# Two of five graph passes: VectorE's part written out, one comparison for four one-hots, waits by fours, eight PSUM banks

## What is computed

```python
# layer 0 (the reference multiplies by the matrix first; the kernel sums first and multiplies then)
support = x @ hamilton
msgs = edge_weight[:, None] * support[edge_src]
out = jax.ops.segment_sum(msgs, edge_dst, num_segments=N)
# layer 4
msg = xw[src] * norm[:, None]
out = jax.ops.segment_sum(msg, dst, num_segments=N) + b
```

## Time and profile before

| | us |
|---|---|
| median of 3 timed executions | 6917.32 (6915.71 to 6927.64) |
| the profiled execution, from first to last instruction | 8185.9 |
| busy in it: PE / PEld | 4889.8 / 3073.8 |
| busy in it: DVE / ACT / POOL | 4369.9 / 2515.7 / 4642.4 |

### The profile page before, as it was taken

The page is one execution under the profiler, slowest core; times in us unless marked ns, Lnnn a source line. Parts: engine busy times, 40 slices in busy tenths (PEclk is TensorE's granted clock), DMA queues, the critical chain, the costliest instruction groups (busy, mean ns, idle before and its releaser), DMA issues. The chain is left out here.

```text
span 8185.9 us, 104343 instructions
## 1 busy us (share of the span) xinstructions
PE 4889.8 (60%) x17264; PEld 3073.8 (38%) x17265; DVE 4369.9 (53%) x11401; ACT 2515.7 (31%) x7600; POOL 4642.4 (57%) x5272
## 2 busy tenths in 40 slices
PE   3555555967777777836565556455555563554555
PEld 1322333534444444624343334233333342332333
DVE  4444444657777777735555556344444452443446
ACT  0000000347777777634444446111111130000003
POOL 5666666445555555556666664555555536666661
PEclk6666666967667777867676678566666676666666
DMA  2323234366666666543333343333333343332234
GB/s 78 89 86 87 86 89 83 125 193 201 194 200 202 196 199 201 138 125 108 106 109 105 103 108 81 95 101 98 100 94 97 95 118 89 88 89 85 86 88 88
DMA packets 499271, 962.78 MB, mean 118 GB/s; under 512 B 105402, under 2 KB 296605, under 8 KB 491711
## 3 DMA queue, kind: packets, MB, share of 16 engines
q0 software_dynamic: 240064, 696.46, 31.0%
q1 hardware_dynamic: 258845, 263.03, 10.4%
HBM read 895.84 MB, written 64.63 MB: 117 GB/s over the span
## 5 line engine op out<-in xcount | busy, mean ns | idle before, releaser
L1026 PE MATMUL bank<-ring,ohc 128*128 128x256 f32 (+3 forms) x8800 | 3440.9, 538 | 2067.8 <-issue 668.3
L1026 PEld LDWEIGHTS bank<-ring,ohc 128*128 128x128 f32 x8800 | 2047.9, 258 | 3233.8 <-issue 1852.1
L1509 DVE TENSOR_TENSOR acc<-acc,bank 128x256 f32 (+2 forms) x3520 | 1483.0, 421 | 1992.4 <-issue 910.1
L711 POOL DMA_INDIRECT ring<-g_t,stage x1760 | 1738.9, 988 | 1149.1 <-PE bank L1026 600.0
L711 POOL DMA_INDIRECT ring<-kv_t,stage x880 | 850.4, 966 | 798.9 <-PE bank L1026 478.2
L711 POOL DMA_INDIRECT ring<-in_x,stage x880 | 835.0, 949 | 483.5 <-issue 229.9
L711 POOL DMA_INDIRECT ring<-xs_t,stage x880 | 834.1, 948 | 473.2 <-issue 227.9
L826 ACT ACTIVATE ring<-ring 128x32 f32<-128x32 f32 x3520 | 754.4, 306 | 15.0 <-issue 14.9
L795 ACT ACTIVATE ohc<-iota,rel_c 128x128 f32<-128x128 f32 x1760 | 564.2, 388 | 183.4 <-PE bank L1026 130.9
L849 ACT ACTIVATE cl<-cl 128x1 f32<-128x1 f32 (+3 forms) x111 | 22.5, 203 | 1863.3 <-issue 883.7
L1506 DVE SCALAR_TENSOR_TENSOR acc<-acc,aux,bank 128x264 f32 x880 | 419.8, 477 | 83.8 <-PE bank L1026 42.7
(11 more groups left out here) (309 smaller groups left out, 5433.5 us busy)
## 6 DMA issues: line engine op xcount, KB each, us to landing
aux<-relb_t SPq DMA_DIRECT2D x56, 1024.0 KB
aux<-q_t SPq DMA_DIRECT2D x880, 64.0 KB
relx<-relb_t SPq DMA_DIRECT2D x55, 512.0 KB
ring<-g_t,stage POOLq DMA_INDIRECT x1760
x<-ring SPq DMA_DIRECT2D x21, 896.0 KB, 4.2
ring<-x SPq DMA_DIRECT2D x21, 896.0 KB, 9.4
mk<-mk SPq DMA_DIRECT2D x445, 32.1 KB
ring<-in_x,stage POOLq DMA_INDIRECT x880
```

The lines of the kernel that those rows point to most:

```text
L711: g_.indirect_dma_start(out=rings[L][:, slot, 0:W], out_offset=None, in_=table[L][:, :], in_offset=bass.IndirectOffsetOnAxis(ap=stage[:, s ...
L1026: return mm(agp[k % AB][:, 0:width], ohc[:, hot, :], rg[:, slot, vo:vo + width], start=True, stop=True)
L1509: tt(win, win, agp[k % AGP[L]][:, 0:width], ALU.add).then_inc(p["added"], 1)
```

## The change

It touches the passes of layers 0 and 4 on DVE and PE. DVE's part is no longer a loop: 220 groups of four tiles are written out, with constant addresses and wait values (only the window's offset still comes from a register). One TENSOR_TENSOR compares `iota` with four columns of `rel_c` and makes four one-hots (128x512). In layer 0 a second one multiplies them by four columns of `ew_c`, after a wait on a new semaphore, `compared`. DVE waits for the matmuls of a group at once, makes the comparison of the group two ahead, adds the four windows and then, in layer 0, multiplies. `LEAD` is now 2 groups instead of 3 tiles, and all 16 buffers of `ohc` are in use. PE keeps its loop and waits by groups for one-hots and banks; it uses eight banks instead of four. In the other layers only the counts of `added` are shifted by four.

```diff
-LEAD = 3
+LEAD = 2
...
-    return sum(TS[m] + LEAD for m in range(L) if HEADS[m] == 0)
+    return sum(TS[m] // 4 for m in range(L) if HEADS[m] == 0)
...
-        AGP = [4, 3, 4, 4, 4]
+        AGP = [8, 3, 4, 4, 8]
...
                         for k in range(G):
-                            pe.wait_ge(p["wready"], b * G + (k + 1 + made_before(L)))
                             slot = rset * G + k
                             if k % 4 == 0:
+                                pe.wait_ge(p["wready"], b * (G // 4) + (k // 4 + 1 + made_before(L)))
                                 pe.wait_ge(s_ring[slot // 4], i * 64 + (64 + ring_base(L, slot // 4)))
-                            pe.wait_ge(p["added"], b * G + (k + 1 + summed(L)))
-                            window_sum(slot, k % 8, k).then_inc(p["agg"], 1)
+                                pe.wait_ge(p["added"], b * G + (k + 4 + summed(L)))
+                            window_sum(slot, k % OHS, k).then_inc(p["agg"], 1)
...
-                    dve.sem_inc(p["added"], 4)
+                    dve.sem_inc(p["added"], 8)
...
                 if not H:
-                    def hot(b, k):
-                        rel = rel_c[:, ds(b * G + k, 1)]
-                        if L == 0:
-                            ins = v.tensor_scalar(ohc[:, k % 8, :], iota[:, :], rel, ew_c[:, ds(b * G + k, 1)],
-                                                  ALU.is_equal, ALU.mult)
-                        else:
-                            ins = v.tensor_scalar(ohc[:, k % 8, :], iota[:, :], rel, None, ALU.is_equal)
-                        ins.then_inc(p["wready"], 1)
...
+                    four = lambda col: col.unsqueeze(2).to_broadcast([128, 4, 128])
+
+                    def hot_four(g):
+
+                        hots = ohc[:, 4 * g % OHS:4 * g % OHS + 4, :]
+                        ins = tt(hots, iota[:, :].unsqueeze(1).to_broadcast([128, 4, 128]),
+                                 four(rel_c[:, 4 * g:4 * g + 4]), ALU.is_equal)
+                        ins.then_inc(s_cmp if L == 0 else p["wready"], 1)
+
+                    def weigh_four(g):
+
+                        hots = ohc[:, 4 * g % OHS:4 * g % OHS + 4, :]
+                        dve.wait_ge(s_cmp, g + 1)
+                        tt(hots, hots, four(ew_c[:, 4 * g:4 * g + 4]), ALU.mult).then_inc(p["wready"], 1)
+
+                    def add_four(g):
+
+                        for k in range(4 * g, 4 * g + 4):
+                            dve.wait_ge(p["added"], k + 8 + summed(L))
+                            win = acc[:, ds(window_at(k // G % 2, k % G), width)]
+                            tt(win, win, banks[k % 8][:, 0:width], ALU.add).then_inc(p["added"], 1)
+                    quads = TS[L] // 4
+                    load_offsets(0, 0, 0)
+                    for g in range(LEAD):
+                        hot_four(g)
+                        if L == 0:
+                            weigh_four(g)
+                    for g in range(quads):
+                        if g % (G // 4) == 1 and (g // (G // 4) + 1) * G < TS[L]:
+                            load_offsets(g // (G // 4) + 1, (g // (G // 4) + 1) % 2, 0)
+                        dve.wait_ge(p["agg"], 4 * g + 4 + 16 * AHEAD[L])
+                        if g + LEAD < quads:
+                            hot_four(g + LEAD)
+                        add_four(g)
+                        if L == 0 and g + LEAD < quads:
+                            weigh_four(g + LEAD)
```

More of the change, by code:

```diff
@@ L350, in gnn_kernel @@
         s_mkst = sem("masks_stored")
+        s_cmp = sem("compared")
         s_same = sem("same_loaded")
@@ L1024, in window_sum @@
                 def window_sum(slot, hot, k):
-                    return mm(agp[k % AB][:, 0:width], ohc[:, hot, :], rg[:, slot, vo:vo + width], start=True, stop=True)
+                    return mm(banks[k % AB][:, 0:width], ohc[:, hot, :], rg[:, slot, vo:vo + width], start=True, stop=True)
                 if not H:
@@ L1058, in add_tiles @@
                                     pe.wait_ge(p["wv"], b * (G // 4) + (weighed(L) + k // 4 + 1))
-                            free = 4 if L == 1 and k == 0 else 5 - AB
+                            free = 8 if L == 1 and k == 0 else 9 - AB
                             pe.wait_ge(p["added"], b * G + (k + free + summed(L)))
@@ L1503, in add_window @@
                     dve.wait_ge(p["agg"], b * G + (k + 1 + 16 * AHEAD[L]))
-                    dve.wait_ge(p["added"], b * G + (k + 4 + summed(L)))
+                    dve.wait_ge(p["added"], b * G + (k + 8 + summed(L)))
                     if L == 1:
@@ L1730, in begin_sums @@
                     def begin_sums(c, off, cp):
-                        dve.wait_ge(p["added"], c * G + (4 + summed(L)))
+                        dve.wait_ge(p["added"], c * G + (8 + summed(L)))
                         dve.wait_ge(p["w"], c + (past(L) + 3))
```

## The result

The changed kernel takes 6962.95 us (6953.71 to 6969.3, four executions) against 6922.05 us for the kernel before beside it: a ratio of 1.0059, interval 1.0047 to 1.0071. It is 0.6% slower, on the side that was forecast and inside the range, but by 41 us where 81 were foretold. A repeat later gave 6962.07 against 6914.35 us, 1.0073 [1.0059, 1.0086].

What follows compares the result with a forecast made beforehand. POOL's gathers were taken to bound both linear passes once DVE doesn't crawl. 6917 us less 30 for the crawl plus 111 for collisions gave 6998 us, 1.2% slower; range 6870 to 7150, the forecast's own 6935 to 7110.

Steps and rivals of the forecast that it cites:

- POOL as the bound: Layers 0 and 4: only POOL's gathers bound the passes if DVE doesn't crawl; DVE and PE work stays hidden, 0 mid-pass.
- The floors: Pass lengths without DVE's crawl, from 880 gathers (1100 us) plus start and end: 1124 us layer 0, 1108 us layer 4.
- The crawl belongs to the profiling: DVE's slow register steps in layers 0 and 4, 479 us when profiled, come from recording; timed kernel keeps 0 to 59.
- The term of -30 us: Layers 0 and 4: the part of DVE's crawl assumed in timed executions, which the change would remove: 30 us.
- the crawl is real: Rival, chance 0.16: DVE crawls in layers 0 and 4 unprofiled too; timed kernel loses 479, pays 111: 6549 us.
- The collision: Layers 0 and 4: wide DVE instructions with two SBUF operands hold POOL's gathers that start inside them: 74 + 37 = 111 us.
- the factor of 0.24 us per us: Gather time lost per us of wide DVE instruction, from layer 2: 69 us on 285 us of L1721.
- Locked in phase: Rival, chance 0.06: every new wide DVE instruction could meet a gather's start, costing 370 us: 7257 us.
- No collision: Rival, chance 0.10: new DVE instructions fall between gather starts or don't hold them: 6887 us, 6858 to 6917.
- the cover is elsewhere: Rival, chance 0.06: POOL's unprofiled pitch is below 1.22 us, PE bounds the pass, collisions cost nothing: 6917 us.

Runs made afterwards that it cites:

- single one-hots: Changed kernel with comparison and multiplication replaced by the old one-hots, one tile each; eight banks, waits by fours and written-out program stay: 6927.83 us, 1.0011 to before.
- the two relatives: Changed kernel with the comparison behind the four adds (0.9897, 0.9872 to before), or split into two of two tiles (0.9899, 0.9904), on chips with the crawl.
- operands in PSUM: Changed kernel with iota and edge weights copied into PSUM banks, so each wide instruction has one SBUF operand; sums share four banks: 6913.38 us, 0.9991 to before.
- the doubled comparison: Changed kernel with each comparison made twice, the second into a buffer that nobody reads: 7030.94 us, 1.0161 to before.
- layer 2's edit: Kernel before with layer 2's L1721 reading weights from their PSUM bank, two preparation steps made ahead of the next scores: 8544.01 us, 1.0152 to before.

## Why the prediction was right, and where not

**POOL as the bound: right.** In the changed kernel POOL waits 7.7 and 0.7 us for PE. Groups of four, late adds and eight banks were to cost nothing in the middle of a pass and up to 3 us at its end. The single one-hots show 4.7 and 2.4 us in all, 2.1 and 1.4 of it at the ends.

**The floors: short by 4 and 18 us.** 1124 and 1108 were forecast, 1128 and 1126 measured. The 55 copies of indices on POOL (11.6 and 11.9 us, `stage` L701) were forgotten, and an end takes 17 us in the kernel before (18 and 20 in the changed one), not 8; in layer 0 the wait of 16.4 us for PE at the start, taken over from the crawling profile, was 5.3.

**"The crawl belongs to the profiling": wrong.** This was the choice on which everything hung. The argument from the two lengths, that an execution 18% longer than the timed ones carries something which these don't, was sound; that this something is the recording was not. The likeliest reading now is that the profile came from a chip with the crawl and the times from one without. Executions without it, profile and all, were seen on two chips, and executions with it on two others. The term of -30 us, what the timed kernel would keep of the crawl, was 0: on the chips of the result there was none to take away. The forecast that the profile would shrink to 7818 us while the time grows was right only in its signs: it shrank to 6958, and the other stages with it.

**The rival "the crawl is real"** (0.16, 6549 us) was nearer the truth than the number of the result says. It holds on two of the four chips; even there the two relatives that were run recover about 1%, not the 5% that it was given; the changed kernel itself wasn't run on such a chip.

**The collision: mechanism right, size 2.2 times too large.** 111 us were forecast, 74 + 37 (worked out exactly, 0.241 us per us gives 73 + 36); the gathers' means say 26 + 21 = 47 against the kernel before, 55 against the same program with operands in PSUM, the excess of the gathers that start inside a wide instruction adds up to 50, and the time says 41 to 50. That the total came as near as 81 against 41 us is partly luck: the 30 us for a crawl that wasn't there took off half of what the collision had too much. The term that failed is the factor of 0.24 us per us, taken over from layer 2 as a whole. Two things are wrong with it.

The smaller one is the form. In layer 2, in the profile from which the forecast was made, gathers that start inside L1721 lose 0.134 us per instruction of the 512 form but 0.346 us per one of the 1024 form, which is 1.8 times as long and makes up almost half of its busy time. By the 512 form alone, the sum would have been 660 x 0.134 = 88 us.

The larger one, the other 38 us or so, is the phase. Each comparison lost 0.09 us in layer 0 and 0.10 in layer 4, each multiplication 0.04, though all have the 512 form's length. In layer 2 POOL and DVE fall into step: held gathers and the instructions of L1721 follow at the same pitch of 1.5 us, and so one gather after another starts at the same place behind an L1721. The rows that follow show it, with 0.29 and 0.30 us between the two starts:

```profile
4138.93 0.68 DVE L1721 TENSOR_TENSOR ring<-ring 128x512 f32<-128x512 f32 x1
...
4139.22 1.21 POOL L711 DMA_INDIRECT ring<-g_t,stage  x1 [0.30 <-issue]
...
4140.44 0.68 DVE L1721 TENSOR_TENSOR ring<-ring 128x512 f32<-128x512 f32 x1
...
4140.74 1.20 POOL L711 DMA_INDIRECT ring<-g_t,stage  x1 [0.30 <-issue]
```

There 131 gathers were held by the 220 instructions of this form, and more than half of them had started 0.30 or 0.31 us behind one. In the changed kernel 53 and 56 were held by 220 comparisons, by 0.37 and 0.40 us each, and 62 by 220 multiplications, but by 0.13 each, since these gathers start only 0.41 us or more behind the multiplication's start. "Locked in phase" is thus half true, and in a mostly harmless phase: 83 and 63 comparisons have a gather that starts between 0.13 us ahead of them and 0.06 us into them, and such a gather loses nothing. That a gather "seems held until its end", less some 0.12 us, as the prediction's bounds have it, was right. Means of 1030 and 990 were forecast for the two layers; 981 and 975 came. That the two are nearly equal shows that the multiplication, which made layer 0 dear in the forecast, was cheap.

The Trainium skill (SBUF — State Buffer, Who interferes with whom) infers that tensor_tensor does not stall descriptor generation. The run with operands in PSUM speaks against that for these gathers: 981 ns with two SBUF inputs, 947 with one, at the same number and length of wide instructions. Its statement that two SBUF inputs contend with a GpSimd instruction that reads SBUF agrees with these numbers.

**"No collision"** (0.10) and **"the cover is elsewhere"** (0.06) are ruled out by the PSUM run and the doubled comparison: time follows the gathers' means in both directions.

## What to carry to other kernels

Before explaining idle time in a profile, compare its span with the timed executions, and profile the same kernel again on another chip if they differ; only then subtract. Where POOL's indirect gathers are the bound, look at each DVE instruction with two operands in SBUF for gathers that start inside it, and count what was left of it, less 0.13 us, as lost; put one operand into PSUM where a bank is free, which took 50 us off here. A factor taken from another stage carries over neither across forms nor across phases. Fewer and wider instructions on an engine that waits anyway bring nothing here, and wide ones with both operands in SBUF hold the bounding engine longer.

## What the hardware showed that was not expected

Four chips ran the same kernel before, at 6917.55, 6914.35, 8418.81 and 8165.5 us (the last two are the long chips below), each within 1% in its own executions. In the two profiles of its loop on a long chip, that of the earlier trace rows and that with layer 2's edit, register, branch and semaphore instructions of DVE, PE, ACT and SP take 0.70 us each for whole stretches, on DVE of 13 and 11 us (medians), instead of a median of 0.03 to 0.05. POOL's are never so long, and a gather's commonest length is 946 ns there, as in some profiles of the short chips. The packets that load the program's instructions are as many with the crawl as without (337 in the profile of the earlier trace rows and in that of the same kernel without it) and as short (median 0.38 us in both), so these packets don't show it. What causes it wasn't tried.

At the end of a pass PE still works for 16 us after the last gather was issued. In the 20 us from 1225 on, in layer 0 of the changed kernel, the DMA engines are busy for seven tenths or more of 25 of the 30 slices until they stop, where the pass as a whole has a share of 0.39. The row is their mean busy share in 40 slices of 0.5 us, in tenths:

```profile
DMA  9799798969779895697999798793850000000000
```

In three quarters of it 1.15 MB were moved, 77 GB/s against 103 in the pass. These last tiles' transfers are slower than POOL's pitch; why was not tried.
